# Attention maxima: the position bias of one pair of heads added by VectorE from a table by queries, and the arguments of GpSimd's roots made on GpSimd

## The reference, cut to what matters

```python
xn = _layernorm(x, ln1_g, ln1_b)                       # x: (32, 256, 128)
q, k, v = jnp.split(xn @ in_proj_w.T + in_proj_b, 3, axis=-1)
mask = _causal_mask(s, rel_pos)                        # one bias for each head, query and key; -inf above the diagonal
scores = jnp.einsum('bhqd,bhkd->bhqk', q, k) / np.sqrt(HD) + mask[None]
attn = jax.nn.softmax(scores, axis=-1)
o = jnp.einsum('bhqk,bhkd->bhqd', attn, v)
x = x + o_projected
xm = _layernorm(x, ln2_g, ln2_b)
mlp = jax.nn.relu(xm @ w1.T + b1) @ w2.T + b2
```

## Time and profile before

| what | value |
|---|---|
| time, median of 3 executions | 1423.78 us (1423.7 to 1432.5) |
| span of the profiled execution | 1524.2 us |
| PE, DVE, ACT, POOL busy share of that span | 80%, 75%, 63%, 65% |
| instructions | 38116 |

### The profile page before, as it was taken

One profiled execution on the slowest core, in us unless ns is written; L12 is line 12 of the kernel. 1 busy time (PEld: TensorE's weight loads), 2 busy tenths in 40 slices (PEclk: granted clock), 3 DMA queues, 4 the chain that ended last, 5 costly groups with the idle time before them and its releaser, 6 DMA issues. The chain is left out here.

```text
span 1524.2 us, 38116 instructions
## 1 busy us (share of the span) xinstructions
PE 1216.6 (80%) x11689; PEld 1017.3 (67%) x11689; DVE 1144.1 (75%) x3833; ACT 967.7 (63%) x2078; POOL 991.9 (65%) x1131
## 2 busy tenths in 40 slices
PE   5889999999999999973788888577787449888850
PEld 3667777777777777753788888455566348788850
DVE  5489999999999999965566665488888546666638
ACT  3588888888888888851555544277777435455420
POOL 4346688888888888777355665237777835666530
PEclk9699999999999999995799997588878669999955
DMA  7211111111111111123222222112222122222228
GB/s 199 86 46 46 48 60 60 60 60 60 59 60 60 60 60 60 39 93 83 73 86 86 81 85 68 49 49 83 73 83 69 45 68 84 86 84 84 77 83 277
DMA packets 99443, 117.19 MB, mean 77 GB/s; under 512 B 17784, under 2 KB 79792, under 8 KB 99248
## 3 DMA queue, kind: packets, MB, share of 16 engines
q1 hardware_dynamic: 70560, 73.57, 16.3%
q0 software_dynamic: 16896, 35.16, 6.8%
q10 hardware_dynamic: 11792, 6.05, 1.4%
HBM read 47.56 MB, written 41.51 MB: 58 GB/s over the span
## 5 line engine op out<-in xcount | busy, mean ns | idle before, releaser
L1153 DVE TENSOR_TENSOR ebuf<-score_banks,region 128x768 f32<-128x768 f32 x256 | 243.6, 951 | 18.8 <-PE score_banks L862 13.1
L1402 ACT ACTIVATE region<-ebuf 128x768 f32<-128x768 f32 x256 | 215.9, 860 | 23.0 <-DVE ebuf L1153 23.0
L1380 ACT CAST copied<-max_banks 128x768 bf16<-128x768 f32 x251 | 201.9, 804 | 15.1 <-PE max_banks L850 12.5
L1842 POOL DMA_INDIRECT choice_rows<-second_yo,second_xg x136 | 133.1, 979 | 112.7 <-PE second_by L1880 69.3
L1842 POOL DMA_INDIRECT choice_rows<-first_yo,first_xg x136 | 130.7, 961 | 114.0 <-PE first_by L1880 65.9
L1694 POOL DMA_INDIRECT expert_rows<-d_rows,a_d_index x112 | 129.4, 1155 | 27.9 <-issue 17.2
L1918 ACT ACTIVATE second_silu<-second_bgu,second_biases 128x256 f32<-128x256 f32 (+1 forms) x144 | 61.0, 466 | 114.3 <-PE second_bgu L1871 66.7
L1918 ACT ACTIVATE first_silu<-first_bgu,first_biases 128x256 f32<-128x256 f32 (+1 forms) x144 | 61.9, 462 | 111.8 <-issue 83.6
L1954 DVE SCALAR_TENSOR_TENSOR second_hT<-second_bgu,second_biases,second_silu 128x256 f32<-128x256 f32 (+1 forms) x144 | 62.1, 464 | 70.3 <-ACT second_silu L1918 37.6
L905 PE MATMUL bankO<-region,vaug 128*32 128x256 f32 (+1 forms) x2048 | 111.1, 334 | 1.9 <-ACT region L1402 1.9
L853 PE MATMUL max_banks<-region_r 32*128 32x256 f32 x502 | 98.3, 388 | 11.9 <-DVE ebuf L1153 7.4
(11 more groups left out here) (369 smaller groups left out, 4531.6 us busy)
## 6 DMA issues: line engine op xcount, KB each, us to landing
region_r<-region_r SPq DMA_DIRECT2D x192, 128.0 KB
first_xg<-expert_rows SPq DMA_DIRECT2D x64, 132.0 KB
second_xg<-expert_rows SPq DMA_DIRECT2D x64, 132.0 KB
z_rows<-choice_rows SPq DMA_DIRECT2D x32, 256.0 KB
c_rows<-choice_rows SPq DMA_DIRECT2D x16, 512.0 KB
out<-xres ACTq DMA_DIRECT2D x16, 256.0 KB
choice_rows<-first_yo,first_xg POOLq DMA_INDIRECT x136
choice_rows<-second_yo,second_xg POOLq DMA_INDIRECT x136
```

Source lines behind the costliest of these rows:

```text
L1153: nc.vector.tensor_tensor(ebuf[:, half_of_ebuf(c, j), :, :], score_banks[:, :, 0:BK], bias32[:, plain(j), :], ALU.add).then_inc(scores_fre ...
L1380: nc.scalar.copy(copied[:, 2 * j:2 * j + 2, :], banks_of_max(c, j)[:, :, 0:BK]).then_inc(maxed_free, 1)
L1402: nc.scalar.activation(p32[:, j % 4, :, :], ebuf[:, half_of_ebuf(c, j), :, :], ACT.Exp).then_inc(exped, 1)
L1842: pool.indirect_dma_start(choice_dram, bass.IndirectOffsetOnAxis(ap=xg[:, i % G, t, E:E + 1].bitcast(I32), axis=0), yo[:, i % 4, t, :], No ...
```

## The change

For pair 3 alone (`MAX_ON_DVE`), TensorE no longer puts the bias into `max_banks`, and ScalarE no longer copies the sum. Instead VectorE adds the bank and a bfloat16 table `bias_by_queries` in one instruction that writes `copied` (`add_for_max`, placed between `finish` and `members`). The table is made once before the first body: six matmuls into `bankO`, a copy by VectorE. The four small VectorE instructions that added epsilon are gone; GpSimd makes `arg` and `arg2` itself from the variances, with three small instructions per body, and the root of the third norm (`row_root`) is taken in the same instruction as the two of the first (`roots`, 6 columns wide where it was 4).

```diff
+    MAX_ON_DVE = (3,)
+    bias_rows = sb("bias_by_queries", [P, 2 * len(MAX_ON_DVE), BK], BF16)
...
             def bias_for_max(c, j):
...
                 if some(copied):
                     pe.wait_ge(maxed_free, copied)
-                for hh in range(2):
...
+                if j not in MAX_ON_DVE:
+                    turn_bias(banks_of_max(c, j), j)
...
             def for_max(c, n, j, second):
-                                                ks[n][rows(h), h // 4, 0:P], start=False, stop=True, skip_group_check=True)
+                                                ks[n][rows(h), h // 4, 0:P], start=alone, stop=True, skip_group_check=True)
...
+            for q, j in enumerate(MAX_ON_DVE):
+                if q:
+                    pe.wait_ge(rows_taken, q)
+                turn_bias(bankO, j).then_inc(rows_full, 1)
             for b in BODIES:
+                if b == 0:
+                    pe.wait_ge(rows_taken, len(MAX_ON_DVE))
                 body(b)
...
             def norm_moments(c, n):
-                    last = ch.mark(nc.vector.bn_aggr(mv[:, n, t, :], stats[:, t, :]))
-                ch.wait(last)
-
-                if some(c):
-                    dve.wait_ge(rs1_ready, c)
-                nc.vector.tensor_scalar(arg[:, 0, :], mv[:, n, :, 1], 1.0, EPS, ALU.mult, ALU.add)
-                nc.vector.tensor_scalar(arg[:, 1, :], mv[:, n, :, 1], 1.0 + EPS, EPS * EPS, ALU.mult, ALU.add).then_inc(arg1_ready, 1)
+                    nc.vector.bn_aggr(mv[:, n, t, :], stats[:, t, :]).then_inc(mv_ready, 1)
...
+            def add_for_max(c, j):
+                if not exists(c):
+                    return
+                dve.wait_ge(maxed_full, 8 * c + j + 1)
+                if some(8 * c + j):
+                    dve.wait_ge(maxed_free, 8 * c + j)
+                if some(c):
+                    dve.wait_ge(folded, len(FOLDS) * (c - 1) + fold_of(j) + 1)
+                at = slice(2 * MAX_ON_DVE.index(j), 2 * MAX_ON_DVE.index(j) + 2)
+                nc.vector.tensor_tensor(copied[:, 2 * j:2 * j + 2, :], banks_of_max(c, j)[:, :, 0:BK], bias_rows[:, at, :],
+                                        ALU.add).then_inc(maxed_free, 1)
...
             def second_moments(c):
-                nc.vector.tensor_scalar(arg2[:], mv2[:, :, 1], 1.0, EPS, ALU.mult, ALU.add).then_inc(arg2_ready, 1)
+                    nc.vector.bn_aggr(mv2[:, t, :], stats2[:, t, :]).then_inc(mv2_ready, 1)
...
             def row_moments(c):
-                nc.vector.tensor_scalar(arg3[:], mv3[:, :, 1], 1.0, EPS, ALU.mult, ALU.add).then_inc(arg3_ready, 1)
+                    nc.vector.bn_aggr(mv[:, row_slot(c), 2 + t, :], stats3[:, t, :]).then_inc(mv3_ready, 1)
...
                 finish(b - 3)
+                add_for_max(b + 1, 3)
                 members(b - 5)
                 row_stats(b - 3)
...
+            for q in range(len(MAX_ON_DVE)):
+                dve.wait_ge(rows_full, q + 1)
+                nc.vector.tensor_copy(bias_rows[:, 2 * q:2 * q + 2, :], bankO[:, :, 0:BK]).then_inc(rows_taken, 1)
+            dve.wait_ge(rows_taken, len(MAX_ON_DVE))
...
             def copy_for_max(c, j):
                 act.wait_ge(maxed_full, 8 * c + j + 1)
+                if j - 1 in MAX_ON_DVE:
+                    act.wait_ge(maxed_free, 8 * c + j)
...
                 exponentials(b - 1, 7)
-                copy_for_max(b + 1, 3)
                 exponentials(b, 0)
...
+            def roots(c, r):
+                    ch.mark(nc.gpsimd.tensor_scalar(arg[:, 4:6], mv[:, n, 0:2, 1], 1.0 + EPS, EPS * EPS, ALU.mult, ALU.add))
...
+                ch.step(nc.gpsimd.tensor_scalar(arg[:, lo:hi], mv[:, n, lo:hi, 1], 1.0, EPS, ALU.mult, ALU.add))
...
+                nc.gpsimd.tensor_tensor(rs[:, n, lo:hi], arg[:, lo:hi], neghalf[:, lo:hi], ALU.pow).then_inc(rs_ready, 1)
...
             def second_root(c):
-                pool.wait_ge(arg2_ready, c + 1)
+                pool.wait_ge(mv2_ready, 2 * c + 2)
+                ch.step(nc.gpsimd.tensor_scalar(arg2[:], mv2[:, :, 1], 1.0, EPS, ALU.mult, ALU.add))
                 nc.gpsimd.tensor_tensor(rs2[:], arg2[:], neghalf[:, 0:2], ALU.pow).then_inc(rs2_ready, 1)
...
-                row_root(b - 3)
                 norm_apply(b + 3, (b + 3) % RING)
-                roots(b + 4, (b + 4) % RING)
+                if exists(b + 4) or exists(b - 3):
+                    roots(b + 4, b - 3)
```

More of the change, by code:

```diff
@@ L665, in attention @@
     xmhi, xmlo = sb("xmhi", [P, 2 * P], F32R), sb("xmlo", [P, 2 * P], F32R)
-    stats3, mv3, arg3, rs3 = sb("stats3", [P, 2, 6]), sb("mv3", [P, 2, 2]), sb("arg3", [P, 2]), sb("rs3", [P, 2])
+    stats3 = sb("stats3", [P, 2, 6])
     dT = sb("dT", [P, 2 * P])
@@ L744, in banks_of_max, with fold_of @@
         return score_banks if g < EARLY and g % 2 == 1 else max_banks
+    def fold_of(j):
+        return sum(j >= past for first, past in FOLDS)
     def group(c):
@@ L814, in max_T, with turn_bias @@
                 nc.tensor.matmul(bankTW[0:H, 0, P:2 * P], mx[:, 0, :], identb[:], start=True, stop=True).then_inc(T_full, 1)
+            def turn_bias(banks, j):
+                for hh in range(2):
+                    h = 2 * j + hh
+                    nc.tensor.matmul(banks[:, hh, 0:P], biasb[:, h, P:2 * P], identb[:], start=True, stop=False,
+                                     skip_group_check=True)
+                    nc.tensor.matmul(banks[:, hh, P:2 * P], biasb[:, h, 0:P], identb[:], start=False, stop=False,
+                                     skip_group_check=True)
+                    last = nc.tensor.matmul(banks[:, hh, 2 * P:BK], biasb[:, h, 0:P], identb[:], start=False, stop=False,
+                                            skip_group_check=True)
+                return last
             def bias_for_max(c, j):
@@ L1182, in second_norm @@
                 dve.wait_ge(W_free, useW("att", c) + 1)
+                if some(c):
+                    dve.wait_ge(mv2_ready, 2 * c)
                 for t in range(2):
@@ L1190, in second_moments @@
                 for t in range(2):
-                    last = ch.mark(nc.vector.bn_aggr(mv2[:, t, :], stats2[:, t, :]))
-                ch.wait(last)
-                if some(c):
-                    dve.wait_ge(rs2_ready, c)
-                nc.vector.tensor_scalar(arg2[:], mv2[:, :, 1], 1.0, EPS, ALU.mult, ALU.add).then_inc(arg2_ready, 1)
+                    nc.vector.bn_aggr(mv2[:, t, :], stats2[:, t, :]).then_inc(mv2_ready, 1)
             def finish(c):
@@ L1376, in copy_for_max @@
                 act.wait_ge(maxed_full, 8 * c + j + 1)
-                g = sum(j >= past for first, past in FOLDS)
-                if some(c) and j == FOLDS[g][0]:
+                if j - 1 in MAX_ON_DVE:
+                    act.wait_ge(maxed_free, 8 * c + j)
+                g = fold_of(j)
+                if some(c) and j == min(i for i in range(*FOLDS[g]) if i not in MAX_ON_DVE):
                     act.wait_ge(folded, len(FOLDS) * (c - 1) + g + 1)
@@ L1573, in _ @@
             ch = Chain(pool, gchain)
-            def roots(c, n):
-                if not exists(c):
-                    return
-                pool.wait_ge(arg1_ready, c + 1)
-                if some(c - RING + 1):
-                    pool.wait_ge(xn_ready, c - RING + 1)
-                    pool.wait_ge(xl_ready, c - RING + 1)
-                nc.gpsimd.tensor_tensor(rs[:, n].rearrange("p a t -> p (a t)"), arg[:].rearrange("p a t -> p (a t)"),
-                                        neghalf[:], ALU.pow).then_inc(rs1_ready, 1)
+            def roots(c, r):
+                n, lo, hi = c % RING, 0 if exists(c) else 2, 4 if exists(r) else 2
+                if exists(c):
+                    pool.wait_ge(mv_ready, 2 * c + 2)
+                    if some(c - RING + 1):
+                        pool.wait_ge(xn_ready, c - RING + 1)
+                        pool.wait_ge(xl_ready, c - RING + 1)
+                    ch.mark(nc.gpsimd.tensor_scalar(arg[:, 4:6], mv[:, n, 0:2, 1], 1.0 + EPS, EPS * EPS, ALU.mult, ALU.add))
+                if exists(r):
+                    pool.wait_ge(mv3_ready, 2 * r + 2)
+                    if some(r - RING + 1):
+                        pool.wait_ge(d_normed, r - RING + 1)
+                ch.step(nc.gpsimd.tensor_scalar(arg[:, lo:hi], mv[:, n, lo:hi, 1], 1.0, EPS, ALU.mult, ALU.add))
+                hi = 6 if exists(c) else hi
+                if hi == 6 and not exists(r):
+                    ch.mark(nc.gpsimd.tensor_tensor(rs[:, n, 4:6], arg[:, 4:6], neghalf[:, 4:6], ALU.pow))
+                    hi = 2
+                nc.gpsimd.tensor_tensor(rs[:, n, lo:hi], arg[:, lo:hi], neghalf[:, lo:hi], ALU.pow).then_inc(rs_ready, 1)
             def norm_apply(c, n):
@@ L1652, in residuals @@
                                         xb2[:].rearrange("p t e -> p (t e)"), ALU.add).then_inc(ysum_ready, 1)
-            def row_root(c):
-                if not exists(c):
-                    return
-                pool.wait_ge(arg3_ready, c + 1)
```

(3 more changed lines are left out.)

47 lines of the change are left out of this document (22 added, 25 removed).

## The result

The changed kernel takes 1459.71 us (median of 4 executions, 1455.05 to 1462.56) against 1424.1 us before (1423.7 to 1432.5): a ratio of 1.0227, 95% interval 1.0191 to 1.0264. It is 2.3% slower. The forecast was 1456, in a range of 1418 to 1470.

A forecast was written before the change was run, and what follows sets the result against it. No engine had much to spare; TensorE's fill 1 was taken to be on the path setting the period. 36.0 over 31 bodies, minus 3.9, plus 2 gave +34, scaled to +32: 1456 us, own range 1444 to 1465, 8-in-10 range 1418 to 1470.

The forecast's parts named there:

- Fill 1 waits for the add: TensorE's first bias matmul of fill 1 waits for VectorE's 0.95 us add; scores 1.16 us later per body, 1.6 idle.
- Who waits then: VectorE's next add_mask waits about 0.5 us for fill 1's scores, where it waited 0.21; turn still waits about 0.65.
- The body: Attention loop: each of 31 bodies 1.16 us longer, less 0.25 in half of them; period about 1 us longer.
- VectorE's four small instructions: Epsilon instructions removed: the first norm's two save 0.25 us, only in bodies of the second kind; the others gain nothing.
- GpSimd: Its changed small instructions add 0.2 to 1.5 us a body, covered by 2.4 idle; xm not late, so no loss.
- The table, +2 us once: Before the first body, VectorE waits for six matmuls and copies 128x768, delaying the start by about 2 us, once.
- The scaling by 0.934: The +34 us of the profiled execution was multiplied by 1423.78 / 1524.2 = 0.934, median over span, giving +32.
- The delay came in full: Rival: fill 1 is not held back and only the savings remain: 14.5 us faster, 1409; chance 0.12.
- absorbed at `turn`: Rival: TensorE's 0.65 us gap at turn absorbs part of the delay, leaving 0.51: +13, 1437; chance 0.14.
- The clock that falls: Rival: TensorE's new idle of 1.6 us per body lowers its clock to 0.88: +36 more, 1491; chance 0.06.
- the 9 us of each body: In the clock rival, the part of a body where TensorE sets the pace, 1.2 us longer at clock 0.88.

The follow-up runs named there:

- e10: Changed kernel with add_mask of pair 0 and finish before take_q, VectorE's step of pair 3 ahead of them, only copying; TensorE keeps the six bias matmuls: 1426.68 us, 1.0004.
- e8: The kernel before, run once more without any edit for its profile: 1426.88 us, with a span of 1425.2.
- e1: Changed kernel without VectorE's add: all eight pairs keep bias matmuls and ScalarE copy, GpSimd makes its roots' arguments: 1423.33 us, 0.9977 of before.
- e2: Kernel before plus VectorE's add of pair 3 and the table; epsilon instructions stay on VectorE: 1465.56 us, 1.0281 of before.
- e7: Changed kernel, but TensorE keeps the six bias matmuls of pair 3 and VectorE only copies the bank at the add's place: 1452.53 us, 1.0180 of before.
- e3: As e1, plus a same-size VectorE sum of a bias tile with itself at the add's place, which nobody reads: 1438.96 us, 1.0101 of before.

## Why the prediction was right, point by point

- **Fill 1 waits for the add.** Right, with its size. I put the first bias matmul of fill 1 at 313.20 - 308.92 = 4.28 us behind `project_q`; it is 309.67 - 305.39 = 4.28. The add takes 0.948 (I took 0.95), and the rule of the Trainium skill that I cited for PSUM operands holds here. TensorE's idle is 1.42, not 1.6, because one term was too large: I had TensorE reach fill 1 sooner by the 0.44 that the six matmuls take, and `weigh` came 0.33 sooner (2.00 behind `project_q`, before 311.25 - 308.92 = 2.33). The scores of fill 0 start 0.53 behind `project_q` (305.92 - 305.39), where the first bias matmul started 0.43 behind it; what holds them for that tenth stays open. From fill 0 on nothing is lost, and e10 measures the same matmuls at 0.32. That changes nothing in the changed kernel, as the add sets the time.
- **Who waits then.** VectorE waits 0.53 for the scores of fill 1 (about 0.5 forecast) and at `take_low_xm` without `arg3` to fill it, ScalarE's freed time is idle, `turn` waits its 0.65.
- **The body.** 1.16 less half of 0.25 is 1.03 us on average; measured are 20.44 - 19.38 = 1.06. The loop from the first `add_mask` to the last is 36.7 us longer (646.5 and 609.8): 31 x 1.06 = 33, and some 4 in its first bodies, which I had not foreseen (last section).
- **VectorE's four small instructions.** 0.125 us a body forecast, 0.08 and 0.14 measured in the two pairs that differ by this half of the change. The place was right too: bodies take 19.2 and 19.6 us in turn in e8, and 19.24 and 19.35 in e1, so the 0.25 comes off the second kind alone.
- **GpSimd.** Nothing forecast, nothing seen; e1 and e2 show it.
- **The table, +2 us once.** The first `take_q` comes at 36.6 instead of 34.2 (34.7 in the first profile of before):

```profile
L1092 DVE SCALAR_TENSOR_TENSOR region_r<-bankTW,bqk,region_r x32: 475/484/485, 34.2 to 617.3; 128x256 fp32r<-128x256 f32 x32
```

```profile
L1108 DVE SCALAR_TENSOR_TENSOR region_r<-bankTW,bqk,region_r x32: 478/484/485, 36.6 to 654.1; 128x256 fp32r<-128x256 f32 x32
```

(the `take_q` line with its first and last start, of e8_before_again and of the changed kernel).
- **The scaling by 0.934.** Wrong, though it cost little. The sum was +34 us; I multiplied it by the median over the span as if that execution had been stretched everywhere. e8 shows that its loop was not stretched. Unscaled, the forecast is 1458, the measured loss 35.6. That the total came out within 4 us is in part luck: what lies behind the last `add_mask`, which no edit touches, takes 744.5 us in the profile of the changed kernel, 754.6 in e8 and 765.1 in e1, so the bodies are the better test. A span that differs by 7% from the median should have been divided among the stages before anything was scaled.
- **The rivals.** The delay came in full, and was not absorbed at `turn`, where the gap is unchanged. The clock that falls did not come: it is 1.00 in the changed kernel from 120 to 680 us, with the wait of 1.4 in every body. No run shows the 9 us of each body in which I let TensorE set the pace.

## What to carry to other kernels

Work given to an engine with idle time elsewhere in its list can cost more than its length, if a busy engine's next step waits for it: follow the chain from the last thing that both engines wait for, not the busy shares. Here the same change came to -0.6% with the add at one place of VectorE's list and to +2.3% with it four instructions later. When such a step is placed, put it first among the work that can run in an existing wait, together with whatever the waiting engine needs next, and look at which bank or buffer is now freed later.

## What the runs showed of the hardware that was not expected

TensorE's granted clock settles at 2.4 GHz (1.00) only some way into the loop, and not at the same time in each profile. Here are windows of the loop's start, columns as in rows 2, first of e8_before_again, then of the changed kernel, then of the first profile of the kernel before:

```profile
60.00:80.00 20.00, 15.21 (x207) 10.79 (x206) 15.01 (x28) 14.99 (x24) 7.16 (x9) 0.86 0.16 53
80.00:100.00 20.00, 16.87 (x232) 12.02 (x232) 17.05 (x37) 17.69 (x30) 9.24 (x13) 1.00 0.17 56
100.00:120.00 20.00, 18.62 (x241) 14.67 (x242) 18.32 (x44) 17.68 (x32) 10.38 (x15) 1.00 0.14 48
```

```profile
60.00:80.00 20.00, 14.21 (x158) 9.98 (x157) 13.50 (x23) 12.18 (x20) 7.19 (x12) 0.66 0.13 43
80.00:100.00 20.00, 16.70 (x204) 12.13 (x201) 15.22 (x30) 14.29 (x25) 4.53 (x9) 0.83 0.13 43
100.00:120.00 20.00, 16.59 (x204) 12.38 (x204) 16.21 (x34) 15.21 (x28) 10.89 (x18) 0.91 0.13 43
```

```profile
60.00:80.00 20.00, 16.48 (x184) 11.52 (x182) 14.02 (x26) 15.06 (x24) 7.15 (x9) 0.74 0.13 45
80.00:100.00 20.00, 17.58 (x238) 12.06 (x236) 17.44 (x38) 16.31 (x27) 6.64 (x9) 0.91 0.16 54
100.00:120.00 20.00, 18.89 (x246) 14.71 (x247) 17.57 (x39) 17.95 (x31) 10.51 (x16) 1.00 0.16 54
```

Shares under 1.00 are a mix of the levels of 1.2 and 2.4 GHz. The changed kernel's profile is the latest of the three, but the two profiles of the kernel before also differ, and e7, whose body has the same length as the changed kernel's, was at 1.00 from 80 us on. So it is not shown that the change delays the rise.

What the late rise goes with can be read by comparing with e7. Its loop took 639.8 us from the first `add_mask` to the last, 6.7 less than the changed kernel's 646.5, and most of that lies in three bodies at the start: 56.5 us from the `take_q` at 61.76 to 118.27 in e7, 61.9 from 61.21 to 123.06 in the changed kernel. Behind the loop it is the other way round (748.9 and 744.5), so the two profiled spans differ by 2.0 alone, and the 7.2 between the medians stay unexplained. Once the clock was up, the wait of 1.4 us in each body did not bring it down in the changed kernel; in e2, with a wait of the same length, it fell once for a moment (0.83 from 370 to 380 us).

The other surprise is the one of e3: a sum of two SBUF tiles on VectorE held up a GpSimd instruction by 0.83 us, the sum of a PSUM bank and an SBUF tile of the same size, at the same place, did not. That the operands are the reason agrees with the section of the Trainium skill cited there; a spare sum with a PSUM operand was not run.
